# A four-layer cross-attention kernel: up products of the small feed-forwards from high and low 16-bit parts

## The reference, cut to what matters

```python
# layer 0, after two int8-like attentions (the second one over the context)
h3 = _ln(x, ln3_g, ln3_b)
hg = h3 @ ff_w1 + ff_b1                      # 128 -> 1024
a, g = jnp.split(hg, 2, axis=-1)
x = a * jax.nn.gelu(g, approximate=False) @ ff_w2 + ff_b2 + x
...
# layer 1, after its cross-attention
h = layer_norm(x, n2_w, n2_b)
h = jax.nn.gelu(h @ fc1_w + fc1_b, approximate=False) @ fc2_w + fc2_b    # 128 -> 512 -> 128
return x + h
```

## Time and profile before

| | |
|---|---|
| median of 3 runs | 968.76 us (967.77 to 968.96) |
| the profiled execution | 973.86 us |
| its span, first to last instruction | 972.0 us |
| mean granted TensorE clock | 0.940 |
| TensorE busy | 861.0 us, 89% |
| VectorE busy | 710.1 us, 73% |
| ScalarE busy | 645.3 us, 66% |
| GpSimd busy | 550.7 us, 57% |

### The profile page before, as it was taken

The page is one execution under the profiler, slowest core; times in us unless marked ns, Lnnn a source line. Parts: engine busy times, 40 slices in busy tenths (PEclk is TensorE's granted clock), DMA queues, the critical chain, the costliest instruction groups (busy, mean ns, idle before and its releaser), DMA issues.

```text
span 972.0 us, 23685 instructions
## 1 busy us (share of the span) xinstructions
PE 861.0 (89%) x8603; PEld 525.0 (54%) x8603; DVE 710.1 (73%) x1555; ACT 645.3 (66%) x1583; POOL 550.7 (57%) x1074
## 2 busy tenths in 40 slices
PE   4989888875675889998999899999889989999996
PEld 2444444443443555555766456655556557776775
DVE  5796888868984666666457667667647887979776
ACT  1888899959995325554356355665446588898985
POOL 2687788877663435663345565666325354646533
PEclk9995999986875999999999799999999999999999
DMA  9500000000000000000000010000000000000000
GB/s 264 183 2 1 1 0 1 2 1 1 1 1 1 1 0 1 2 2 1 1 2 2 22 25 23 23 23 25 1 1 3 1 2 2 2 7 7 7 7 23
DMA packets 23580, 16.48 MB, mean 17 GB/s; under 512 B 8744, under 2 KB 20400, under 8 KB 23344
## 3 DMA queue, kind: packets, MB, share of 16 engines
q1 hardware_dynamic: 23472, 15.06, 5.4%
HBM read 10.85 MB, written 1.05 MB: 12 GB/s over the span
## 4 chain that ended last, share of the span: by engine, by line
PE 62%; DVE 16%; ACT 13%; issue 5%; POOL 3%; DMA 0%; SPq 0%; DVEq 0%; ACTq 0%; POOLq 0%
ACT sb_E L1284 9%; PE ps_context L806 6%; PE ps_context L809 4%; PE ps_scores L906 4%; PE ps_scores L882 4%; PE ps_turned L1184 2%; PE ps_turned L720 2%; PE ps_turned L1185 2%; PE ps_turned L1186 2%; PE ps_scores L1163 2%; PE ps_scores L1161 2%; PE ps_scores L1162 2%; PE ps_scores L759 2%; PE ps_scores L799 2%; PE ps_turned L1121 2%
## 5 line engine op out<-in xcount | busy, mean ns | idle before, releaser
L1284 ACT ACTIVATE sb_E<-ps_scores,sb_neg_max,sb_score_scale 128x256 f32<-128x256 f32 (+1 forms) x384 | 191.0, 514 | 14.9 <-DVE sb_neg_max L1585 9.2
L2348 POOL TENSOR_SCALAR sb_E<-sb_E,sb_inv_sum 128x256 f16<-128x256 f32 x256 | 123.7, 483 | 30.7 <-DVE sb_inv_sum L1621 11.6
L1794 DVE TENSOR_REDUCE sb_neg_half<-ps_scores 128x16 f32<-128x1024 f32 x48 | 58.7, 1223 | 64.4 <-PE ps_scores L882 64.4
L1539 ACT ACTIVATE sb_E<-ps_scores,sb_ff_bias 128x512 f32<-128x512 f32 x128 | 88.8, 693 | 21.9 <-PE ps_scores L1163 17.0
L720 PE MATMUL ps_turned<-sb_ident 128*128 128x512 f16 x289 | 89.3, 430 | 9.5 <-DVE sb_ident_b L2217 9.5
L1604 DVE TENSOR_REDUCE sb_neg_quad<-ps_scores 128x2 f32<-128x512 f32 (+1 forms) x96 | 64.3, 685 | 43.2 <-PE ps_scores L761 31.1
L1312 ACT ACTIVATE sb_E<-ps_scores 128x512 f32<-128x512 f32 x96 | 57.2, 598 | 47.5 <-PE ps_scores L801 46.2
L1411 ACT ACTIVATE sb_E<-ps_scores 128x1024 f32<-128x1024 f32 x48 | 49.2, 1024 | 55.0 <-PE ps_scores L914 55.0
L1580 DVE TENSOR_REDUCE sb_neg_raw<-ps_scores 128x4 f32<-128x1024 f32 x64 | 77.9, 1218 | 8.4 <-PE ps_scores L692 8.3
L1284 ACT ACTIVATION_READ_ACCUMULATOR sb_E<-ps_scores,sb_neg_max,sb_score_scale 128x1 f32 x384 | 79.2, 206 | 0.0
L2279 POOL TENSOR_SCALAR sb_veps<-sb_mv 128x2 f32<-128x2 f32 x72 | 18.4, 255 | 91.8 <-DVE sb_mv L1562 90.9
(11 more groups left out here) (315 smaller groups left out, 2589.9 us busy)
## 6 DMA issues: line engine op xcount, KB each, us to landing
sb_moe_up<-in_moe_up SPq DMA_DIRECT2D x1, 2048.0 KB
sb_KS<-sb_qk_parts SPq DMA_DIRECT2D x96, 16.0 KB, 1.8
sb_QS<-sb_qk_parts SPq DMA_DIRECT2D x96, 16.0 KB, 1.8
sb_rows<-in_rows SPq DMA_DIRECT2D x1, 1216.0 KB, 7.5
out_x<-sb_raw_context SPq DMA_DIRECT2D x8, 128.0 KB, 1.8
sb_X<-in_x SPq DMA_DIRECT2D x1, 768.0 KB, 9.5
sb_square<-in_square SPq DMA_DIRECT2D x1, 768.0 KB, 10.9
sb_ctxT<-in_ctxT SPq DMA_DIRECT2D x1, 512.0 KB, 11.0
```

The costliest lines, as they stand in the source:

```text
L1284: last = act.activation(E[:, ring, head], SC[t % 2][:, head], ACT.Exp, bias=neg_max[:, ring, h:h + 1], scale=scale, accum_out=row_sum[:, r ...
L1539: act.activation(U_full[:, n % RING, :], banks[n % 4], ACT.Gelu, bias=bias, scale=1 / WEIGHT_SCALE)
L1794: dve.tensor_reduce(neg_half[:, n % 2, :, :, :].rearrange("p x i g -> p (x i g)"), SC[0][:, :].rearrange("p (h k) -> p h k", k=CTX), AX.X, ...
L2348: last = pool.tensor_scalar(E16[:, ring, SEQ * h:SEQ * h + SEQ], E[:, ring, SEQ * h:SEQ * h + SEQ], inv_sum[:, ring, h:h + 1], HALF, ALU.m ...
```

## The change

Weights, tokens and products of the two small feed-forwards take the form that the experts' have.

- `split_ff` on GpSimd splits the three up matrices of 128x512 in place, in nine steps; the scratch space is `raw_context`. Six of them stand in the second int8 attention at even steps of `p` = 1 to 3, at the head of GpSimd's step and behind a wait for VectorE's maxima of the same step; the other three at `(4, 2)`. With the first goes a scaling of four bias columns.
- `chunk_hT` writes the tokens in float32 to one buffer, then a cast makes the high part and a subtraction the low part, each behind a wait for the one before; `h_ring` now holds the parts.
- `up` issues three float16 matmuls per product in place of one float32 matmul, and waits once per feed-forward for the splits.
- Gelu takes a scale of 1/64, and the gated feed-forward's `take` scales by 1/64 while it adds.

```diff
-        h_ring = (hT[:, :, :].rearrange("p a k -> p (a k)"), KBD[:, 0, UNIT:2 * UNIT].bitcast(F32))
+        h_ring = (KBD[:, 0, UNIT:2 * UNIT], KBD[:, 1, UNIT:2 * UNIT])
+        h_full = hT[:, :, :].rearrange("p a k -> p (a k)")
+        ff0_parts = ff0_up[:, :].bitcast(F16).rearrange("p (g k) -> p g k", g=2)
+        ff1_parts = ff1_up[:, :].bitcast(F16)
...
+                def product(out, parts):
+                    hi, lo = parts[:, P * k:P * k + P], parts[:, FF + P * k:FF + P * k + P]
+                    pe.matmul(out, hi, h_hi, start=True, stop=False)
+                    pe.matmul(out, hi, h_lo, start=False, stop=False)
+                    return pe.matmul(out, lo, h_hi, start=False, stop=True)
+
                 if k == 0:
+                    if c == 0:
+                        pe.wait_ge(ff_split, 6 if L.gated else 9)
                     wait(pe, S["chunk_hT"], B["chunk_hT"] + c + 1)
...
-                    pe.matmul(dst[:, 512:1024], ff0_up[:, FF + P * k:FF + P * k + P], h, start=True, stop=True)
-                    last = pe.matmul(dst[:, 0:512], ff0_up[:, P * k:P * k + P], h, start=True, stop=True)
+                    product(dst[:, 512:1024], ff0_parts[:, 1, :])
+                    last = product(dst[:, 0:512], ff0_parts[:, 0, :])
                 else:
-                    last = pe.matmul(dst[:, 0:512], ff1_up[:, P * k:P * k + P], h, start=True, stop=True)
+                    last = product(dst[:, 0:512], ff1_parts)
...
-                dve.tensor_scalar(h_ring[c % 2], bank_of(L, "C", c)[:, :], col(L.name + "_g"), col(L.name + "_b"), ALU.mult,
-                                  ALU.add).then_inc(S["chunk_hT"], 1)
+                dve.tensor_scalar(h_full, bank_of(L, "C", c)[:, :], col(L.name + "_g"), col(L.name + "_b"), ALU.mult,
+                                  ALU.add).then_inc(S["h_full"], 1)
+                hi, lo = h_ring[c % 2][:, 0:CHUNK], h_ring[c % 2][:, CHUNK:]
+                dve.wait_ge(S["h_full"], B["h_full"] + c + 1)
+                dve.tensor_copy(hi, h_full).then_inc(S["h_hi"], 1)
+                dve.wait_ge(S["h_hi"], B["h_hi"] + c + 1)
+                dve.tensor_tensor(lo, h_full, hi, ALU.subtract).then_inc(S["chunk_hT"], 1)
...
+                if L.gated:
+                    dve.scalar_tensor_tensor(x, TP[0][:, :], 1 / WEIGHT_SCALE, x, ALU.mult, ALU.add).then_inc(S["taken"], 1)
...
+                if L is A2 and p in (1, 2, 3) and t % 2 == 0:
+                    pool.wait_ge(S["maxed"], B["maxed"] + L.steps * p + t + 1)
+                    split_ff(2 * (p - 1) + t // 2)
+                if L is A2 and (p, t) == (4, 2):
+                    for n in (6, 7, 8):
+                        split_ff(n)
                 if o == L.norm_step and normed:
                     inverse_std(NB, batch, b)
                 normalise(L, B, p, t)
...
+            def split_ff(n):
+
+                i, j = n // 3, n % 3
+                if n == 0:
+                    pool.wait_ge(loaded["ff"], N_LOADS["ff"])
+                    pool.tensor_scalar(ff_bias[:, 0:4], ff_bias[:, 0:4], WEIGHT_SCALE, 0.0, ALU.mult, ALU.add)
+                wait(pool, ff_split, n)
+                parts, scaled = (ff0_parts[:, 0, :], ff0_parts[:, 1, :], ff1_parts)[i], raw_context[:, i % 2, :]
+                if j == 0:
+                    last = pool.tensor_scalar(scaled, parts.bitcast(F32), WEIGHT_SCALE, 0.0, ALU.mult, ALU.add)
+                elif j == 1:
+                    last = pool.tensor_scalar(parts[:, 0:FF], scaled, 1.0, 0.0, ALU.mult, ALU.add)
+                else:
+                    last = pool.tensor_tensor(parts[:, FF:2 * FF], scaled, parts[:, 0:FF], ALU.subtract)
+                last.then_inc(ff_split, 1)
```

More of the change, by code:

```diff
@@ L282, in counts @@
                  taken=NCHUNK * layer.experts)
+        if layer.experts == 1:
+            c.update(h_full=NCHUNK, h_hi=NCHUNK)
         if layer.norm == "post":
@@ L562, in build @@
         weights_split = ctx.enter_context(nc.semaphore("s_weights_split"))
+        ff_split = ctx.enter_context(nc.semaphore("s_ff_split"))
         values_cleared = ctx.enter_context(nc.semaphore("s_values_cleared"))
@@ L1094, in up @@
                 n = L.tiles * c + k
-                dst, h = SC[k % 2], h_ring[c % 2]
+                dst, h_hi, h_lo = SC[k % 2], h_ring[c % 2][:, 0:CHUNK], h_ring[c % 2][:, CHUNK:]
+                def product(out, parts):
[3 more added lines that the diff above has]
+                    return pe.matmul(out, lo, h_hi, start=False, stop=True)
                 if k == 0:
+                    if c == 0:
+                        pe.wait_ge(ff_split, 6 if L.gated else 9)
                     wait(pe, S["chunk_hT"], B["chunk_hT"] + c + 1)
@@ L1508, in activate @@
                     act.activation(act_g[:, k % 2, :], SC[k % 2][:, 512:1024], ACT.Gelu,
-                                   bias=ff_bias[:, 4 + k:5 + k]).then_inc(S["act"], 1)
+                                   bias=ff_bias[:, 4 + k:5 + k], scale=1 / WEIGHT_SCALE).then_inc(S["act"], 1)
                     return
-                act.activation(U_ring[n % 3], SC[k % 2][:, 0:512], ACT.Gelu, bias=ff_bias[:, 8 + k:9 + k])\
+                act.activation(U_ring[n % 3], SC[k % 2][:, 0:512], ACT.Gelu, bias=ff_bias[:, 8 + k:9 + k],
+                               scale=1 / WEIGHT_SCALE)\
                    .then_inc(S["act"], 1)
@@ L1974, in take @@
                 x = chunk_of_x(c)
-                dve.tensor_tensor(x, TP[0][:, :], x, ALU.add).then_inc(S["taken"], 1)
+                if L.gated:
+                    dve.scalar_tensor_tensor(x, TP[0][:, :], 1 / WEIGHT_SCALE, x, ALU.mult, ALU.add).then_inc(S["taken"], 1)
+                else:
+                    dve.tensor_tensor(x, TP[0][:, :], x, ALU.add).then_inc(S["taken"], 1)
             def chunk_of_x(c):
```

## The result

The changed kernel takes 972.79 us (median of 20 runs, 970.44 to 974.79), the kernel before 970.29 us (20 runs beside them): ratio 1.0029, 95% interval [1.0021, 1.0038]. It is slower by 0.29%; the forecast was 966.2 us, the range up to 970.5. Of the 6.6 us between forecast and result 1.5 lie in the starting value (968.76 us from 3 runs, 970.29 from 20); a gain of 2.6 us was forecast, and a loss of 2.5 measured.

What follows compares the result with a forecast made beforehand. TensorE was taken as the bound (62% of the chain, busy 89% of the span). First feed-forward -2.4, second +0.2, extra slack -0.4 give -2.6 us: from 968.76 to 966.2 us, range 963.0 to 970.5.

Steps and rivals of the forecast that it cites:

- Hand-over: Tokens from VectorE to TensorE, both feed-forwards: cast and subtraction make each of 8 chunks 1.2 us later.
- rival C: Between chunk_turn and up: VectorE's hand-over bounds all eight chunks, casts meeting GpSimd; +2.7 us, 971.5; chance 0.09.
- the term for the clock: First feed-forward, chunk 1: after about 3.5 us idle TensorE's clock falls, costing +1.5 us.
- (a): First feed-forward, start to chunk 1: -0.1 us in all, idle time of 2.26 growing to about 3.5.
- (b): First feed-forward, chunk 1 after the idle time: clock falls, +1.5 us, while two tiles give back 0.84.
- (c): First feed-forward, chunk 2's z to the context rows: z meets GpSimd's memset unchanged; two tiles give 0.42 us each.
- (d): First feed-forward, context rows to end: six tiles save 2.5 us, less 0.4 waiting for VectorE's queue.
- F1: forecast +0.2: Second feed-forward: chunk 1 starts 1.7 us later, all 3.4 us of products saved are eaten, ending about 0.2 late.
- rival B: Clock also falls before second feed-forward's chunk 1, or first's starting half clock lasts longer: 967.7, both 969.2; chance 0.23.
- rival D: Second int8 attention: the splits on GpSimd don't fit and push its sums, up to 4.8 us back, 971.0; chance 0.06.
- Rival A: First feed-forward: the clock holds at the longer idle time before chunk 1, about -5.2 us, 963.6; chance 0.22.
- The extra -0.4 for slack: Both feed-forwards: -0.4 us for chunks where VectorE's queue has more slack than the walk allows.

Runs made afterwards that it cites:

- tokens_only: The kernel before with only the tokens' added cast and subtraction; float32 products stay, weights unsplit, the parts unused: ratio 1.0086 to the kernel before.
- products_only: The changed kernel with tokens evicted once, straight to float16, their low part left out; three 16-bit products and weight splits stay: ratio 0.9936 to the kernel before.
- fillers: The changed kernel with TensorE's idle times in both feed-forwards filled by 16-bit products that nobody reads: ratio 0.9997 to the kernel before.
- plain_only: The kernel before with the whole change in the second (plain) feed-forward alone: ratio 0.9999 to the kernel before.
- gated_only: The kernel before with the whole change in the first (gated) feed-forward alone: ratio 1.0061 to the kernel before.

## Why the prediction was wrong

Products: the price was right. Three 16-bit ones start 0.65 us apart from the next three in F0 too (310.29 and 310.94 on the changed kernel's L1105), as in the earlier trace rows.

Hand-over: its size was right (1.18 to 1.19, and casts at 0.43 throughout in the changed kernel, so rival C's collisions with GpSimd did not lengthen them). The prediction counts the cast of the earlier trace rows as evidence against the rule that it cites for them; GpSimd had no instruction beside that cast, so those rows say nothing of it. "The idle times show only about half of the hand-overs on the path" held for the waits: 4.9 of 9.5 us in tokens_only, 5.3 on top of the 16-bit products.

What failed is mostly the term for the clock. The sum has +1.5 for one more fall of it, behind the longer wait before chunk 1 of F0, takes the fall behind the third turn as unchanged, and puts the rest at nothing. Measured were that fall, one behind the third turn of twice the length (some 6 us at half clock for 3), a new one behind the context rows, and a new one in F1. TensorE's busy time says what they cost: less the 10.1 us of the products it should be 80.0 us in F0 and F1, in products_only it is 80.12, and in the changed kernel 86.11. So the clock costs some 6.1 us (an estimate from these sums; fillers, which held it, got 5.9 back, with the one fall that the kernel before has too) where 1.5 stood. The waits were off too, by less: -2.2 was -10.1 + 1.5 and thus 6.4 us of new idle time, and 8.2 came (11.90 to 20.09). The two errors, 4.6 and 1.8, are the 6.4 between -2.2 and +4.2.

The walk through F0, by its steps. (a) forecast -0.1, measured -0.07 (start to chunk 1 in 16.89 us, before 16.96), and the idle time grew to 3.25. (b) forecast +0.66, measured +0.67 (9.74 to 10.41 up to the third turn), the clock falling as said. TensorE's busy time stayed at 7.2 us; the 0.65 are its longer wait for z, which VectorE began later behind the slower tiles. (c) forecast -0.84, measured +1.1 up to the context rows (10.39 to 11.50): this is the step that failed first. Its words that the 1.2 of chunk 2 "lies in VectorE's idle time there" held. VectorE had 2.20 us of it before, and still has 1.66 with the hand-over, waiting for Gelu, as its timelines show (the kernel before, then the changed one):

```profile
341.71 0.75 DVE L1968 SCALAR_TENSOR_TENSOR sb_U<-ps_scores,sb_ff_bias,sb_act_g 128x512 f32<-128x512 f32 x1 [2.20 <-ACT sb_act_g L1508]
```
```profile
337.00 0.75 DVE L1989 SCALAR_TENSOR_TENSOR sb_U<-ps_scores,sb_ff_bias,sb_act_g 128x512 f32<-128x512 f32 x1 [1.66 <-ACT sb_act_g L1523]
```

What came late was the tile that Gelu waits for. Its six 16-bit products ran wholly at half clock and took 2.56 us (333.47 to 336.03), more than the two float32 ones before (338.83 to 340.78, 1.95). The gate followed 6.14 us behind the third turn, before 5.50, and the context rows came after 2.65 us of idle time, with another fall of the clock behind them; before it was 2.15 and no fall, as TensorE's timeline shows:

```profile
346.60 0.66 PE L838 MATMUL ps_context<-sb_ident,sb_ctx_rows 128*128 128x128 f32 x4 [2.15 <-DVE sb_ctx_rows L2250]
```

(d) forecast -2.1, measured +0.26 up to the fourth turn and -0.43 from there to X1 (20.07 to 19.64). The prediction counts one tile up to the fourth turn, and there are two (L1105 at 347.10 and 349.71 before). Behind it the clock was full in both kernels, so here it is the waits: TensorE is busy 1.85 us less, and 1.4 of them turned into idle time, with new waits for VectorE of 0.67 and 0.86 us and VectorE busy 16.53 of 19.64 us. The earlier trace rows showed 15.41 of 20.1 there; with 1.2 more on VectorE and 2.1 less on TensorE VectorE has little slack left.

F1: forecast +0.2, measured +2.69. Chunk 1 starts 1.85 later, as said (1.7); then the clock fell at 2.24 us of idle time (some 1.6 us: plain_only, where it held, is 1.65 shorter), which was the first half of rival B. (Its second half, a longer half clock at the start of F0, didn't come: 6.1 us, before 5.9.) The other 0.8 us are plain_only's +1.04 against the forecast's +0.2, behind the wait for the context's low part (1.63, before 0.22).

Splits (rival D): nothing, as forecast. Rival A (the clock holds) came out only when fillers made it hold, and then at 0.9997. C's sign came out, but not for its reason, longer casts. The extra -0.4 for slack had no ground.

So two causes share the loss: VectorE's 9.5 us, which with three steps take the products' whole saving even in the best order found, and the clock, which makes -1.7 into +4.2 us. They aren't independent, since the falls stand behind waits for VectorE. What stays open is why gated_only was timed 0.45% above what its stages say, and what besides the idle time decides about the clock.

## What to carry to other kernels

When work moves from the bounding engine to its neighbour, price each longer wait twice: once for the wait, and once for the clock that may fall behind it. Here the second price was as large as the first (6.0 and 5.3 us on top of the products), and it was the one missing from the sum. A neighbour that is busy for 77% of a stretch has less slack than it seems. Before making products cheaper, look for idle times that come from the neighbour's order: here statistics, normalisation and set-up steps moved by a few places gave 1.0% without the change, and the change on top gave nothing. And compare two profiles by landmarks, since unchanged code ahead of the second attention took 208.4 to 215.3 us in different profiles.
